# Two heads in two halves of the rows: maxima four at a time, weighing every second slot, other jobs in even slots

## The chip, the cores and the metric

One core of a Trainium2 chip runs the whole program in one launch. The metric is the device time in microseconds of that core. The kernel before took 1429.73 us, the median of three runs (1427.91 to 1433.0). TensorE is the matrix engine, VectorE, ScalarE and GpSimd work on rows, SyncE (SP) issues the DMAs. Matmuls write to PSUM, which has eight banks of 512 f32 columns on 128 partitions.

## The reference

Six blocks run one after the other on x (4 x 256 tokens of 256) with a context of 4 x 4096 tokens of 128. Only the first matters here, attention of x to the context with 16 heads of 16 columns:

```
qh = (q @ Wq + bq) by heads          # q: the normalized x, 256 queries per batch
kh = (k @ Wk + bk) by heads          # k: 4096 context tokens per batch
vh = (v @ Wv + bv) by heads
scores = einsum('bhqd,bhkd->bhqk', qh, kh) / sqrt(16)
attn = softmax(scores)
out = einsum('bhqk,bhkd->bhqd', attn, vh)
```

The five blocks behind it are not touched.

## The kernel before

**Exact products from bf16.** A query or key is split into three bf16 parts (high, middle, low; 16 rows each for a head). Six of the nine products of parts are wanted. They are laid under each other in the rows: 6 x 16 = 96 rows of queries and of keys for a head, read from DRAM by three DMAs for blocks of 48, 32 and 16 rows (`RUNS`, L1019 for keys, L1005 for queries). Two more rows hold minus the maximum of each query, against ones in the keys, so that a matmul of 98 rows gives shifted scores.

**Groups and slots.** A group is two heads of a batch; there are 32. A group has 16 slots, a slot 256 keys (two tiles of 128, `e2`), so there are 512 slots. The numbers t of slots also run from -60 to -1 ahead of them, where keys, queries and first maxima are made. In every slot each engine goes through the same list of work in its own loop over t (`tensor`, `vector`, `scalar`, `gpsimd`, `sync`), with semaphores between them:

- *Scores* (L540): for a tile of keys, two matmuls of 98x256, one for each head, into one bank. Three banks (0 to 2) go round by half-slots. ScalarE's exponential (L783) of 128x512 empties a bank into `probs`.
- *Maxima* (L524): a matmul of 96 rows, 128 queries by 512 keys; VectorE takes the maximum of each row (L685). They run 19 slots ahead, two in a slot, one behind the first scores and one behind the second. When all 32 maxima of a group are there, VectorE finds the shift, TensorE turns it (L614), and ScalarE copies it into the query rows (L846).
- *Weighing* (L559): values (17 columns with a column of ones) times probabilities in f32, in four groups of 32 columns of the array, for four slots at once, in every fourth slot, into bank 3.
- *Other jobs*, at slots that `plan` writes in a table (`due`): keys of the next units projected (L587) and split by GpSimd, values projected (L626), context turned (L578), gathers of a finished group (L645), the shift (L614), and from slot 412 on jobs of the next block ("stream").

**Banks of maxima and jobs.** From slot -1 on a maximum or a job takes the next of banks 4 to 7 in turn (`misc` in `tensor`). Its first matmul waits until the holder before has been emptied, for a maximum by VectorE's `peaked`, for a job mostly by a copy on ScalarE.

**SP** issues loads and stores in the order of the same table; `read keys` brings 1.5 MB for a group into one of three buffers, 31 slots ahead of it.

A matmul in f32 is two instructions in the trace. "96*128" in a row is rows by columns of the weights.

Of the kernel before, what the change touches and what calls it, by code (L numbers as in the profile page):

```python
# [14 lines left out]
P = 128  # L15
# [282 lines left out]
PAIRS = 6  # L298
ROWS = PAIRS * DH
AUG = ROWS + 2  # L300
# [10 lines left out]
HALVES, SUMS = 3, 3  # L311
# [4 lines left out]
class ContextAttention0:  # L316
# [12 lines left out]
    def __init__(self, k, scope):  # L329
# [12 lines left out]
        self.keysT = sb(scope, "keysT", [P, RING, GH, LC], BF16)  # L342
        self.values = [values, sb(scope, "values1", [P, LC // P, H, DH + 1])]
        self.queriesT = sb(scope, "queriesT", [P, 2, P // DH, S], BF16)
# [17 lines left out]
        self.q_dram = k.nc.dram_tensor("q_parts0", (B, P // DH, PARTS, DH, KD, S), BF16).ap()  # L362
# [20 lines left out]
        self.max_made, self.peaked, self.scored, self.exped = sig("max_made"), sig("peaked"), sig("scored"), sig("exped")  # L383
# [6 lines left out]
    def plan(self):  # L390
# [31 lines left out]
        for u in range(2, B * KD):  # L422
            b, m = divmod(u, KD)
            for c in range(CH):
                slot = UNIT * u - 101 + 8 * c
                if m == 0:
                    at(slot - 15, "load ctx", b, c)
                    at(slot, "turn ctx", b, c)
                    at(slot + 6, "save ctx", b, c)
                at(slot + 2, "fill keys", u, c)  # L430
                if c % 2:
                    at(slot + 7, "write parts", u, c // 2)
# [22 lines left out]
    def maxima(self, t):  # L455
# [5 lines left out]
        return range(made(t - 1), made(t))  # L461
# [36 lines left out]
    def tensor(self, e, w):  # L498
# [13 lines left out]
        def find_max(n, now):  # L512
            i, r = divmod(n, MAXES)
            pair, c = self.max_at(n)
            j, t = divmod(pair, QT)
            u, g = divmod(i, UNIT_GROUPS)
            job, let_go = ("max", n), (self.peaked, n)
# [4 lines left out]
            else:  # L522
                w.wait_ge(self.pieces_here[c * self.PIECES // CH], 0)
            e.matmul(ps, self.queriesT[0:ROWS, u % 2, g * GH + j, t * P:(t + 1) * P],  # L524
                     self.keysT[0:ROWS, i % RING, j, c * BANK:(c + 1) * BANK],
                     start=True, stop=True).then_inc(*self.max_made.up(n))

        for t in range(FIRST, TOTAL + 3):
# [16 lines left out]
            if t % 4 == 1 and 5 <= t <= TOTAL + 1:  # L545
                i, p0 = divmod(t - 5, SLOTS)
                b, g = divmod(i, NG)
                w.wait_ge(self.exped, (t - 2, 1))
                for p in range(p0, p0 + 4):
# [5 lines left out]
                for p in range(p0, p0 + 4):  # L555
                    for e2 in range(2):
                        for j in range(GH):
                            quad, kt = e2 * GH + j, 2 * p + e2
                            made = e.matmul(k.bank(SUMS)[32 * quad:32 * quad + DH + 1, 0:S],  # L559
                                            self.values[b % 2][:, kt, g * GH + j, :],  # L560
                                            self.probs[:, (SLOTS * i + p) % RINGP, quad * S:(quad + 1) * S],
                                            start=(p == 0), stop=(p == SLOTS - 1))
                made.then_inc(*self.weighed.up((t - 5) // 4))
            for n in maxima[1:]:
                find_max(n, t)

            for job, *a in self.due.get(t, ()):
# [40 lines left out]
                elif job == "turn shift":  # L608
# [4 lines left out]
                    for pair in range(GH * QT):  # L613
                        made = e.transpose(ps[ROWS:AUG, pair * P:(pair + 1) * P], self.shift_b[:, i % 2, pair, :],  # L614
# [20 lines left out]
    def max_at(self, n):  # L635

        i, r = divmod(n, MAXES)
        return divmod(r, CH) if i else divmod(r, GH * QT)[::-1]
# [30 lines left out]
    def vector(self, e, w):  # L669
# [11 lines left out]
        def peak(n):  # L681
            i, r = divmod(n, MAXES)
            pair, c = self.max_at(n)
            w.wait_ge(self.max_made, n)
# [2465 lines left out]
```

## Time and profile before

| | |
|---|---|
| median of three runs | 1429.73 us (1427.91 to 1433.0) |
| profiled execution, span | 1429.1 us, 28070 instructions |
| slots 0 to 415 | 67.06 to 788.66 us |
| slots 416 to 511 | 788.66 to 963.2 us |
| TensorE, VectorE, ScalarE, GpSimd busy | 96%, 74%, 65%, 20% |
| DMA | 133.19 MB, mean 93 GB/s |

The only time that the profile has of the profiled execution is its span; the median of the runs is 0.6 us above it. A busy share counts matmuls from start to a modelled end, and ends overlap the next starts, so the pitch from start to start says what a matmul costs. In a row of the timeline equal instructions are merged: its second number runs from the first start to the last end. What stands in brackets is the idle time before it and what ended it.

### The profile page before, as it was taken

The numbers are of one execution on the slowest core, as the hardware profiler recorded it, in microseconds if no ns is written. First come the engines' busy times: TensorE is split into PE (matmuls) and PEld (weight loads), VectorE is DVE, ScalarE is ACT, GpSimd is POOL, SyncE is SP. The second block draws the span as 40 slices with busy tenths as digits, with TensorE's granted clock in tenths as the row PEclk, the third lists the DMA queues.
The fourth block names the chain that finished last, engine by engine and source line by source line (L and its number), as shares of the span: only waits on it lengthen the run. The fifth ranks groups of instructions, "written<-read, shape, count | busy, mean of one in ns | idle before, by whom it ended". The sixth has DMA issues, their size and how long they took to land.

```text
span 1429.1 us, 28070 instructions
## 1 busy us (share of the span) xinstructions
PE 1375.6 (96%) x11138; PEld 846.7 (59%) x11138; DVE 1055.1 (74%) x2114; ACT 922.1 (65%) x1899; POOL 287.6 (20%) x321
## 2 busy tenths in 40 slices
PE   7799999999999999999999999999999999989998
PEld 5355555555555545555554556556557999856666
DVE  4787777787777778777778888835876778767757
ACT  5366777767777767777767666672796664448731
POOL 3354222222222222122213100000003100001210
PEclk9899999999999999999999999999999999999999
DMA  6966555346554545655454743002402320347000
GB/s 184 163 145 143 119 118 111 77 102 130 116 127 92 102 84 125 128 115 113 81 97 101 184 73 61 2 1 60 119 18 65 112 67 1 91 112 155 2 1 30
DMA packets 95587, 133.19 MB, mean 93 GB/s; under 512 B 8864, under 2 KB 70944, under 8 KB 89504
## 3 DMA queue, kind: packets, MB, share of 16 engines
q1 hardware_dynamic: 95456, 131.40, 42.3%
q8 instruction: 88, 1.44, 0.5%
q14 instruction: 43, 0.35, 0.1%
HBM read 94.15 MB, written 37.22 MB: 92 GB/s over the span
## 4 chain that ended last, share of the span: by engine, by line
PE 79%; ACT 8%; DVE 8%; DMA 2%; issue 2%; SPq 1%; POOL 0%; DVEq 0%; ACTq 0%
PE psum L559 16%; PE psum L540 13%; PE psum L524 13%; ACT probs L783 4%; PE psum L2132 4%; PE psum L587 3%; PE psum L2106 3%; DVE peaks L685 3%; PE psum L626 3%; PE psum L1226 2%; PE psum L2851 2%; PE psum L1623 1%; PE psum L275 1%; PE psum L2861 1%; PE psum L2814 1%
## 5 line engine op out<-in xcount | busy, mean ns | idle before, releaser
L685 DVE TENSOR_REDUCE peaks<-psum 128x1 f32<-128x512 f32 x1024 | 643.3, 684 | 197.0 <-PE psum L524 196.4
L783 ACT ACTIVATE probs<-psum 128x512 f32<-128x512 f32 x1024 | 529.0, 615 | 83.3 <-PE psum L540 79.4
L524 PE MATMUL psum<-keysT,queriesT 96*128 96x512 bf16 x1024 | 390.1, 384 | 13.2 <-DMA keysT<-key_parts 7.9
L540 PE MATMUL psum<-queriesT,keysT 98*128 98x256 bf16 x2048 | 392.4, 274 | 6.1 <-ACT queriesT L846 2.4
L540 PEld LDWEIGHTS psum<-queriesT,keysT 98*128 98x128 bf16 x2048 | 176.3, 99 | 191.7 <-ACT probs L783 72.1
L559 PE MATMUL psum<-probs,values 128*17 128x256 f32 x4096 | 245.9, 380 | 0.0
L559 PEld LDWEIGHTS psum<-probs,values 128*17 128x17 f32 x4096 | 107.2, 97 | 102.6 <-issue 27.1
L524 PEld LDWEIGHTS psum<-keysT,queriesT 96*128 96x128 bf16 x1024 | 98.6, 96 | 90.9 <-issue 56.1
L918 POOL CAST key_parts<-key_f 128x512 bf16<-128x512 f32 x57 | 34.8, 611 | 518.0 <-ACT key_f L816 511.0
L816 ACT ACTIVATE key_f<-psum,bk 128x512 f32<-128x512 f32 x59 | 40.5, 687 | 120.7 <-PE psum L587 120.6
L587 PE MATMUL psum<-ctxT,wk 128*128 128x512 f32 x128 | 69.5, 625 | 2.4 <-DVE probs L728 0.9
L924 POOL TENSOR_TENSOR key_parts<-key_r,key_parts 128x512 bf16<-128x512 f32 x57 | 66.0, 1158 | 4.5
L920 POOL TENSOR_TENSOR key_r<-key_f,key_parts 128x512 f32<-128x512 f32 x57 | 65.9, 1157 | 4.5
L2132 PEld LDWEIGHTS psum<-ctx_nat,ring 128*128 128x128 f32 x512 | 64.6, 191 | 3.6 <-ACT ring L2267 0.7
L2132 PE MATMUL psum<-ctx_nat,ring 128*128 128x129 f32 x512 | 65.9, 275 | 0.7 <-ACT ring L2267 0.6
L626 PE MATMUL psum<-wv,ctxT 128*128 128x256 f32 x256 | 65.4, 381 | 0.5 <-DVE probs L716 0.4
L1919 ACT ACTIVATE weights<-psum,peaks 128x256 f32<-128x256 f32 x128 | 58.7, 487 | 10.5 <-DVE peaks L1788 10.3
L2106 PE MATMUL psum<-early_weights,ctx_T 128*128 128x256 f32 x256 | 63.2, 380 | 0.0
L857 ACT ACTIVATE values<-psum 128x512 f32<-128x512 f32 x64 | 38.0, 599 | 29.3 <-PE psum L626 28.5
L2257 ACT ACTIVATE ring<-psum 128x512 f32<-128x512 f32 x64 | 37.7, 596 | 29.1 <-PE psum L2106 28.8
L626 PEld LDWEIGHTS psum<-wv,ctxT 128*128 128x128 f32 x256 | 47.9, 190 | 14.0 <-issue 5.5
L2267 ACT ACTIVATE ring<-ring 128x1024 f32<-128x1024 f32 (+1 forms) x36 | 34.6, 962 | 24.3 <-DVE ring L2177 24.1
(315 smaller groups left out, 1662.5 us busy)
## 6 DMA issues: line engine op xcount, KB each, us to landing
keysT<-key_parts SPq DMA_DIRECT2D x31, 768.0 KB, 7.7
key_parts<-key_parts SPq DMA_DIRECT2D x90, 256.0 KB
keysT<-key_parts SPq DMA_DIRECT2D x31, 512.0 KB, 10.1
ctx_nat<-in_ctx_dram SPq DMA_DIRECT2D x32, 256.0 KB, 3.0
keysT<-key_parts SPq DMA_DIRECT2D x31, 256.0 KB, 11.6
ctx_in<-in_ctx_dram SPq DMA_DIRECT2D x24, 256.0 KB, 5.9
ctx_turned<-ctxT SPq DMA_DIRECT2D x24, 256.0 KB, 4.4
ctx_T<-ctx_turned SPq DMA_DIRECT2D x12, 512.0 KB, 3.8
```

Source lines behind the costliest of these rows:

```text
L524: e.matmul(ps, self.queriesT[0:ROWS, u % 2, g * GH + j, t * P:(t + 1) * P], self.keysT[0:ROWS, i % RING, j, c * BANK:(c + 1) * BANK], star ...
L540: made = e.matmul(ps[:, j * S:(j + 1) * S], self.keysT[0:AUG, i % RING, j, kt * P:(kt + 1) * P], self.queriesT[0:AUG, u % 2, g * GH + j, : ...
L559: made = e.matmul(k.bank(SUMS)[32 * quad:32 * quad + DH + 1, 0:S], self.values[b % 2][:, kt, g * GH + j, :], self.probs[:, (SLOTS * i + p) ...
L587: e.matmul(ps, self.wk[:, 0, m * P:(m + 1) * P], self.ctxT[:, c * BANK:(c + 1) * BANK], start=True, stop=True).then_inc(*self.key_made.up( ...
L626: made = e.matmul(ps[:, e2 * D:(e2 + 1) * D], self.ctxT[:, kt * P:(kt + 1) * P], self.wv[:, 0, :], start=True, stop=True)
L685: e.tensor_reduce(self.peaks[:, i % 2, pair, c:c + 1], k.ps(("max", n)), AX.X, ALU.max).then_inc(*self.peaked.up(n))
L783: e.activation(self.probs[:, t % RINGP, e2 * GH * S:(e2 + 1) * GH * S], k.ps(("scores", t, e2)), ACT.Exp).then_inc(*self.exped.up((t, e2)))
L920: e.tensor_tensor(self.key_r[:, :], k_f, part(0), ALU.subtract).then_inc(*w.up(self.split_pool, ("rest",) + key))
L924: e.tensor_tensor(part(2), self.key_r[:, :], part(1), ALU.subtract).then_inc(*w.up(self.split_pool, ("part2",) + key))
L1919: made = e.activation(self.weights[:, (2 * q + i) % self.NR, kt, :], k.ps(("scores3", q, i))[:, kt * S:(kt + 1) * S], ACT.Exp, bias=self.p ...
L2106: made = e.matmul(ps[:, i * S:(i + 1) * S], l.ctx_T[:, b % 2, kt * P:(kt + 1) * P], l.qcT[:, b * S:(b + 1) * S], start=True, stop=True)
L2132: made = e.matmul(k.ps(("weigh4", b, i))[:, 0:C + 1], self.at(n)[:, column:column + P], l.ctx_nat(b % 2)[:, kt, :], start=(kt == 0), stop= ...
```

## The change

Names: `MAIN` and `REST` are two planes of the key and query rows. Head j of a group lies in rows 64j to 64j+63. `MAIN` holds four of the six products (64 rows), `REST` the other two (32 rows) and the two shift rows (34 in all).

- Scores: for each tile and head one matmul of 64 rows and one of 34, added up in PSUM; a bank now belongs to a head (both tiles of a slot) and no longer to a tile (both heads). Three banks as before.
- Maxima: the 64 rows of `MAIN` only (the maximum need not be exact, it cancels); four in every even slot, head 0 and 1 in turn, behind all scores.
- Weighing: two slots at once, in every odd slot (`BLOCK`).
- Table: key projections, context and their writes one slot later or earlier, so that they fall on even slots; value projections every eighth slot instead of every sixth.
- The shift is copied by two instructions, one for each head.
- DMAs: keys of a group six of 32 rows each (three before); query parts are written in five copies (three before) and read by four DMAs (three before).

```diff
-            for e2 in range(2):
-                if 0 <= t < TOTAL:
-                    kt, n = 2 * p + e2, (2 * t + e2) % HALVES
-                    ps = banks.use(n, w, ("scores", t, e2), (self.exped, (t, e2)))
-                    for j in range(GH):
-                        made = e.matmul(ps[:, j * S:(j + 1) * S], self.keysT[0:AUG, i % RING, j, kt * P:(kt + 1) * P],
-                                        self.queriesT[0:AUG, u % 2, g * GH + j, :], start=True, stop=True)
-                    made.then_inc(*self.scored.up((t, e2)))
-                if maxima and not e2:
-                    find_max(maxima[0], t)
+                ps = {}
+                for e2 in range(2):
+                    kt = 2 * p + e2
+                    for plane, rows in ((MAIN, HALF), (REST, TALL)):
+                        for j in range(GH):
+                            if j not in ps:
+                                ps[j] = banks.use(SCORES[(2 * t + j) % len(SCORES)], w, ("scores", t, j), (self.exped, (t, j)))
+                            own = slice(j * HALF, j * HALF + rows)
+                            made = e.matmul(ps[j][:, e2 * S:(e2 + 1) * S], self.keysT[own, plane, i % RING, kt * P:(kt + 1) * P],
+                                            self.queriesT[own, plane, u % 2, g, :], start=(plane == MAIN), stop=(plane == REST))
+                            if e2 and plane == REST:
+                                made.then_inc(*self.scored[j].up((t, j)))
+            for n in maxima:
+                find_max(n, t)
...
+        if t < 0:
+            return range(made(t - 1), made(t))
+        return range(made(t - 1), made(t + 1)) if t % 2 == 0 else range(0)
...
-                slot = UNIT * u - 101 + 8 * c
+                slot = UNIT * u - 100 + 8 * c
...
-                at(SLOTS * NG * b - 97 + 6 * p, "make values", b, p)
+                at(SLOTS * NG * b + (8 * p - 96 if p < 12 else (-6, 0, 2, 8)[p - 12]), "make values", b, p)
...
-        for block, run in RUNS:
-            e.dma_start(self.keysT[block * DH:(block + run) * DH, i % RING, :, keys],
-                        self.key_dram[u, g * GH:(g + 1) * GH, PARTS - run:PARTS, :, keys].rearrange(
-                            "j i d n -> (i d) j n")).then_inc(*landed.up(key))
+        for j in range(GH):
+            for row, plane, first in ((0, MAIN, 1), (LOW, MAIN, 1), (0, REST, 0)):
+                e.dma_start(self.keysT[j * HALF + row:j * HALF + row + LOW, plane, i % RING, keys],
+                            self.key_dram[u, g * GH + j, first:first + 2, :, keys].rearrange("i d n -> (i d) n")).then_inc(
+                    *landed.up(key))
```

TensorE, a steady piece with a value projection, before. L540 are scores, L524 maxima, L559 weighing, L626 values; `exped` is ScalarE's exponential, `peaked` VectorE's maximum:

```order
944 L524 MATMUL psum<-keysT,queriesT 128x512 [waits peaked]
945 L540 MATMUL psum<-queriesT,keysT 128x256 [waits exped]
946 L540 MATMUL psum<-queriesT,keysT 128x256
947 L559 MATMUL psum<-probs,values 17x256 x16
948 L524 MATMUL psum<-keysT,queriesT 128x512 [waits peaked]
949 L626 MATMUL psum<-wv,ctxT 128x256 [waits peaked]
950 L626 MATMUL psum<-wv,ctxT 128x256
951 L540 MATMUL psum<-queriesT,keysT 128x256 [waits exped]
952 L540 MATMUL psum<-queriesT,keysT 128x256
953 L524 MATMUL psum<-keysT,queriesT 128x512 [waits peaked]
```

The same kind of piece now (L548 scores, L529 maxima, L568 weighing, L634 values):

```order
694 L548 MATMUL psum<-queriesT,keysT 128x256 [waits exped] x2
695 L548 MATMUL psum<-queriesT,keysT 128x256 x6
696 L529 MATMUL psum<-keysT,queriesT 128x512 [waits peaked] x3
697 L529 MATMUL psum<-keysT,queriesT 128x512 [waits key_kept]
698 L634 MATMUL psum<-wv,ctxT 128x256 [waits peaked]
699 L634 MATMUL psum<-wv,ctxT 128x256
700 L548 MATMUL psum<-queriesT,keysT 128x256 [waits exped] x2
701 L548 MATMUL psum<-queriesT,keysT 128x256 x6
702 L568 MATMUL psum<-probs,values 17x256 x8
703 L548 MATMUL psum<-queriesT,keysT 128x256 [waits exped] x2
```

The single maxima between scores have become a run of four behind a slot's eight score matmuls, the job stands right behind the four, and weighing has half the matmuls and comes twice as often. Both runs of the job wait for `peaked`, but four turns of the banks back is now the first of the four maxima just issued.

SP ahead of slot 0, from the last piece of group 0 to the keys of group 2, before (L1019 keys, L980 ones, L983 x):

```order
34 L1019 DMA keysT<-key_parts 48x2x1024 [waits parts3_out]
35 L1019 DMA keysT<-key_parts 32x2x1024
36 L1019 DMA keysT<-key_parts 16x2x1024
37 L1019 DMA keysT<-key_parts 48x2x4096
38 L1019 DMA keysT<-key_parts 32x2x4096
39 L1019 DMA keysT<-key_parts 16x2x4096
40 L980 DMA keysT<-in_const_dram 1x128x96 x2
41 L983 DMA values<-in_x_dram 128x6x256
```

and now (L1036 keys, L991 ones, L995 x):

```order
34 L1036 DMA keysT<-key_parts 32x1024 [waits parts3_out]
35 L1036 DMA keysT<-key_parts 32x1024 x5
36 L1036 DMA keysT<-key_parts 32x4096 x6
37 L991 DMA keysT<-in_const_dram 1x128x48 x4
38 L995 DMA values<-in_x_dram 128x6x256
```

Each read of keys has twice as many DMAs, with the same places in the row.

## Rows read from the trace of the kernel before

**Rows 1.** The page: busy time of the engines, and the granted clock in 40 slices

```profile
PE 1375.6 (96%) x11138; PEld 846.7 (59%) x11138; DVE 1055.1 (74%) x2114; ACT 922.1 (65%) x1899; POOL 287.6 (20%) x321
...
PEclk9899999999999999999999999999999999999999
```

**Rows 2.** Windows: length, busy by engine, clock, DMA share, GB/s

```profile
67.06:788.66 721.60, 713.80 (x6425) 386.45 (x6423) 549.87 (x1008) 519.90 (x1015) 201.34 (x229) 1.00 0.55 112
...
788.66:963.20 174.54, 168.35 (x1555) 102.32 (x1554) 130.94 (x277) 114.95 (x223) 12.43 (x12) 1.00 0.30 62
```

**Rows 3.** Timeline (start, length, engine) of scores and maxima, around 504 and 509 to 512

```profile
504.35 0.11 PEld L540 LDWEIGHTS psum<-queriesT,keysT 98*128 98x128 bf16 x2 [0.27 <-ACT probs L783]
...
508.60 0.38 PE L540 MATMUL psum<-queriesT,keysT 98*128 98x256 bf16 x2
...
509.04 0.38 PE L540 MATMUL psum<-queriesT,keysT 98*128 98x256 bf16 x2
...
509.26 0.38 PE L524 MATMUL psum<-keysT,queriesT 96*128 96x512 bf16 x1
...
509.48 0.38 PE L540 MATMUL psum<-queriesT,keysT 98*128 98x256 bf16 x2
...
509.94 0.39 PE L540 MATMUL psum<-queriesT,keysT 98*128 98x256 bf16 x2
...
511.04 1.88 DVE L685 TENSOR_REDUCE peaks<-psum 128x1 f32<-128x512 f32 x3
```

**Rows 4.** Timeline of one weighing of four slots

```profile
511.90 0.39 PE L540 MATMUL psum<-queriesT,keysT 98*128 98x256 bf16 x2
...
512.22 1.92 PE L559 MATMUL psum<-probs,values 128*17 128x256 f32 x32
...
514.07 0.39 PE L524 MATMUL psum<-keysT,queriesT 96*128 96x512 bf16 x1
```

**Rows 5.** Timeline: a key projection (two matmuls), a transpose of context (four)

```profile
501.09 1.02 PE L587 MATMUL psum<-ctxT,wk 128*128 128x512 f32 x2
...
340.68 0.60 PE L578 MATMUL psum<-const,ctx_in 128*128 128x128 f32 x4
```

**Rows 6.** Timeline: f32 matmuls alone, then in pairs of row groups; their durations

```profile
1000.81 1.03 PE L1701 MATMUL psum<-early_weights,w_oT 128*128 128x256 f32 x4
...
1001.77 1.13 PE L1623 MATMUL psum<-qT,kT 32*128 32x256 f32 x8
...
L1623 PEld LDWEIGHTS psum<-qT,kT x256: 181/185/333, 978.4 to 1067.7; 32*128 32x128 f32 x128
...
L1623 PE MATMUL psum<-qT,kT x256: 374/374/791, 978.4 to 1068.1; 32*128 32x256 f32 x128
```

**Rows 7.** Timeline: an exponential, a maximum's matmul and its reduction

```profile
503.69 0.61 ACT L783 ACTIVATE probs<-psum 128x512 f32<-128x512 f32 x1
...
507.50 0.39 PE L524 MATMUL psum<-keysT,queriesT 96*128 96x512 bf16 x1
...
507.93 0.69 DVE L685 TENSOR_REDUCE peaks<-psum 128x1 f32<-128x512 f32 x1 [1.07 <-PE psum L524]
```

**Rows 8.** Timeline: a reduction and the load that waits for its bank

```profile
48.04 0.68 DVE L685 TENSOR_REDUCE peaks<-psum 128x1 f32<-128x512 f32 x1
...
48.77 0.10 PEld L524 LDWEIGHTS psum<-keysT,queriesT 96*128 96x128 bf16 x1 [0.50 <-DVE peaks L685]
```

**Rows 9.** Waits: total, times, longest

```profile
PEld psum L645 <- DVE peaks L685: 8.0, 17, 1.6
```

**Rows 10.** Lines, 67.06 to 788.66: count, busy, mean ns, idle before

```profile
L685 DVE TENSOR_REDUCE peaks<-psum 128x1 f32<-128x512 f32 x831 | 522.5, 684 | 168.2 <-PE psum L524 167.9
...
L783 ACT ACTIVATE probs<-psum 128x512 f32<-128x512 f32 x830 | 426.7, 617 | 37.5 <-PE psum L540 34.5
```

**Rows 11.** Timeline: the first maximum of group 1, and SP's reads

```profile
62.10 1.98 PE L524 MATMUL psum<-keysT,queriesT 96*128 96x512 bf16 x4 [6.41 <-DMA keysT<-key_parts]
...
517.31 1.25 SPq L1019 DMA_DIRECT2D keysT<-key_parts  x3
```

More of the change, by code:

```diff
@@ L297 @@
 RUNS = ((0, 3), (3, 2), (5, 1))
-PAIRS = 6
-ROWS = PAIRS * DH
-AUG = ROWS + 2
+KEY_AT = (1, 2, 0)
+QUERY_AT = ((2, 3), (0, 1), (4,))
+HALF = P // 2
+MAIN, REST = 0, 1
+LOW = 2 * DH
+TALL = LOW + 2
 NG = H // GH
@@ L512, in find_max @@
         def find_max(n, now):
-            i, r = divmod(n, MAXES)
-            pair, c = self.max_at(n)
-            j, t = divmod(pair, QT)
+            i, j, qt, c = self.max_at(n)
             u, g = divmod(i, UNIT_GROUPS)
+            own = slice(j * HALF, (j + 1) * HALF)
             job, let_go = ("max", n), (self.peaked, n)
@@ L523, in find_max @@
                 w.wait_ge(self.pieces_here[c * self.PIECES // CH], 0)
-            e.matmul(ps, self.queriesT[0:ROWS, u % 2, g * GH + j, t * P:(t + 1) * P],
-                     self.keysT[0:ROWS, i % RING, j, c * BANK:(c + 1) * BANK],
-                     start=True, stop=True).then_inc(*self.max_made.up(n))
+            e.matmul(ps, self.queriesT[own, MAIN, u % 2, g, qt * P:(qt + 1) * P],
+                     self.keysT[own, MAIN, i % RING, c * BANK:(c + 1) * BANK],
+                     start=True, stop=True).then_inc(*self.max_made[j].up(n))
         for t in range(FIRST, TOTAL + 3):
@@ L637, in max_at @@
         i, r = divmod(n, MAXES)
-        return divmod(r, CH) if i else divmod(r, GH * QT)[::-1]
+        step, j = divmod(r, GH)
+        qt, c = divmod(step, CH) if i else divmod(step, QT)[::-1]
+        return i, j, qt, c
     def gather(self, e, w, ps, i):
@@ L845, in scalar @@
                     w.wait_ge(self.shiftT_made, i)
-                    e.activation(self.queriesT[ROWS:AUG, u % 2, g * GH:(g + 1) * GH, :].rearrange("p h n -> p (h n)"),
-                                 k.ps(("shiftT", i)).bitcast(BF16)[ROWS:AUG, 0:GH * S], ACT.Copy).then_inc(
-                        *self.shiftT_kept.up(i))
+                    for j in range(GH):
+                        own = slice(j * HALF + LOW, j * HALF + TALL)
+                        e.activation(self.queriesT[own, REST, u % 2, g, :], k.ps(("shiftT", i)).bitcast(BF16)[own, 0:S],
+                                     ACT.Copy).then_inc(*self.shiftT_kept.up(i if j else ("first", i)))
                 elif job == "make values":
@@ L978, in sync @@
                     n, first, last = CONST_COLS["ones"]
-                    for r in range(ROWS, AUG):
-                        e.dma_start(self.keysT[r:r + 1, :, :, :].rearrange("o r h n -> o (r h n)").bitcast(F32).rearrange(
-                            "o (p n) -> o p n", p=P), io["const"][:, first:last].unsqueeze(0)).then_inc(*self.ones_in.up(0))
+                    for r in (LOW, LOW + 1, HALF + LOW, HALF + LOW + 1):
+                        e.dma_start(self.keysT[r:r + 1, REST, :, :].rearrange("o r n -> o (r n)").bitcast(F32).rearrange(
+                            "o (p n) -> o p n", p=P), io["const"][:, first:(first + last) // 2].unsqueeze(0)).then_inc(
+                            *self.ones_in.up(0))
                 elif job == "load x":
@@ L989, in sync @@
                     if i >= RING:
-                        w.wait_ge(self.scored, (SLOTS * (i - RING + 1) - 1, 1))
+                        for j in range(GH):
+                            w.wait_ge(self.scored[j], (SLOTS * (i - RING + 1) - 1, j))
                     self.read_keys(e, i, slice(0, LC), self.keys_here[i % RING], i)
@@ L1002, in sync @@
                     if u >= 2:
-                        w.wait_ge(self.scored, (UNIT * (u - 1) - 1, 1))
-                    for block, run in RUNS:
-                        e.dma_start(self.queriesT[block * DH:(block + run) * DH, u % 2, :, :],
-                                    self.q_dram[b, :, 0:run, :, m, :].rearrange("h i d n -> (i d) h n")).then_inc(
-                            *self.rows_here[u % 2].up(u))
+                        for j in range(GH):
+                            w.wait_ge(self.scored[j], (UNIT * (u - 1) - 1, j))
+                    for plane, rows, parts in ((MAIN, HALF, slice(0, 4)), (REST, LOW, slice(3, 5))):
+                        for j in range(GH):
+                            e.dma_start(self.queriesT[j * HALF:j * HALF + rows, plane, u % 2, :, :],
+                                        self.q_dram[b, j::GH, parts, :, m, :].rearrange("h i d n -> (i d) h n")).then_inc(
+                                *self.rows_here[u % 2].up(u))
                 elif job == "load output weights":
```

67 lines of the change are left out of this document (33 added, 34 removed).

## The prediction

> **What bounds the kernel now.** I read the page's shares first: TensorE is busy 96% of the span at full clock, and no other engine is over 74% [rows 1]. The reader should see that "busy" hides waits, so I next cut the span into stretches. The 416 slots from 67.06 to 788.66 us take 721.60 us, 1.735 us a slot, and the last 96 slots 174.54 us [rows 2]. In the first of these TensorE is busy 713.80 us, VectorE 549.87, ScalarE 519.90. The change works here; the 466 us behind 963.2 run code that it does not touch.
>
> Then the timeline of a few slots. A maximum follows every pair of scores, and both take 0.22 us where nothing waits (509.04 to 509.26 to 509.48). From the fourth half-slot on, the pitch grows from 0.44 to 0.49 us, because scores wait for an exponential [rows 3]. Eight half-slots then run from 508.60 to 512.13 us (the second matmul of the pair at 511.90 starts 0.39 - 0.27 = 0.12 later and streams 0.11). Weighing follows: its first load starts at 512.22, 0.09 after the last column, and the next maximum starts at 514.07. So four slots' weighing costs 1.95 us, of which eight waves of 0.216 are work and 0.22 are the two changes of array layout [rows 4]. With the eighth maximum (0.22) four slots cost 3.53 + 0.22 + 1.95 = 5.70 us. 104 such blocks are 593 us, and the other jobs 123 us (52 key projections at 2 x 0.43, 48 value projections at 4 x 0.216, 24 transposes of context and 25 gathers at 4 x 0.11, 26 turns of the shift at 0.32, few others; the counts are the order's, the pitches (1.02 - 0.59) and (0.60 - 0.27) / 3) [rows 5]. That is 716 of 721.60; the method is 0.8% short.
>
> **The change on TensorE.** *Maxima.* 128x512 stays, but the two heads lie in rows 0 to 63 and 64 to 127. Do such pairs run side by side? The trace has pairs in different 32-row groups: eight f32 matmuls start at 1001.77 and end at 1002.90. Less one duration (0.374) the last starts at 1002.53; with the first wave delayed 0.10 by its load, that is 0.216 a pair, where single f32 matmuls of 256 columns have the same pitch ((1.03 - 0.38) / 3) [rows 6]. So I take a pair at the price of one: four maxima cost 0.44 instead of 0.87 us, 0.43 us saved in two slots. *Scores.* Four matmuls a slot become eight, in four waves of 0.11: 0.455 us against 0.45. Nothing saved. *Weighing.* Every second slot: four waves 0.86, plus 0.09 before and 0.11 behind [rows 4]; two layout changes more in four slots, 0.11 us a slot.
>
> *The wait of scores.* Three banks hold scores, and slot t+1 needs for its second head the bank of slot t's first head. Before, a half-slot reused the bank of three half-slots earlier, with maxima in between. Now both heads of a slot finish together. Set the first score load of an even slot at 0: columns end at 0.46; the last wave starts at 0.35, is complete at 0.62, ScalarE starts 0.04 later and takes 0.60 (one exponential 0.61), and TensorE goes on 0.05 after its end (503.69 + 0.61 to 504.35) [rows 3, 7]: 1.31. The maxima fill 0.46 to 0.90, and 0.41 us stay empty. Odd scores then end at 1.77, weighing at 2.85, when the next wait is long over. A pair of slots costs 2.86 us with the first load, against 5.70 / 2 = 2.85 before: the 0.43 saved is spent on a wait of 0.41, and the second layout change is paid by the score waits of before that go.
>
> *The wait of the other jobs.* They take turns with the maxima in four banks. Four maxima at once take all four, so a job in an even slot needs the bank of the first of these very maxima. The first maximum starts at 0.47, is complete at 0.86, VectorE starts 0.04 later (507.50 + 0.39 to 507.93) for 0.69 us, and its bank comes free 0.05 behind it (48.04 + 0.68 to 48.77) [rows 7, 8]: load at 1.63. An f32 load without cover costs 0.10 [rows 6]. Then 0.86 of work and 0.11 to change the layout back: scores at 2.70 instead of 1.31, +1.39, for a job that cost 0.86. Before, the maximum whose bank it took was two slots old; only 8.0 us of such a wait (17 gathers) are in the trace [rows 9]. Transposes or a gather: 1.63 + 0.10 + 0.44 + 0.11 - 1.31 = +0.97; both +1.40; keys and shift +1.81. By the order, of 208 even slots below 416, 48 have values, 25 keys, 25 keys and shift, 25 transposes or a gather, 12 both, one the shift alone (+0.74). That is 67 + 35 + 45 + 24 + 17 + 1 = 189; jobs in odd slots behind weighing 6.
> Sum: 208 x 2.86 + 189 + 6 = 790; with the 0.8% that the method lacks, 796 against 721.6: **+74**. The last 48 pairs: 137 + 30 + 12 (19 of their jobs lie in odd slots, which need no fresh peak), 180 against 174.5: **+5**.
>
> **VectorE and ScalarE.** Maxima back to back come every 0.60 us on VectorE ((1.88 - 0.68) / 2), four take 2.4 us, under 2.86; exponentials cost ScalarE at most 0.51 (426.7 / 830), four 2.1 [rows 3, 10]. Neither bounds. The shift's copy becomes two, on 32 groups, some 0.3 us each, beside idle ScalarE; if not hidden, 10 us.
> The Trainium skill, "TensorEngine Tiling (Array Packing)", section PSUM Bottleneck, warns that tiling speeds up TensorE but not the emptying of PSUM. By that rule alone two slots could not go under VectorE's 2.4 us. The trace agrees that VectorE keeps 0.60 a maximum, but my sum stays above that floor, so here it is latency and not throughput that takes the gain.
>
> **Transfers.** A read of keys becomes six DMAs of 32 rows instead of three, the same bytes. An issue holds SP some 0.43 us (three in 1.25), so +1.3 us a read, with 11 slots to spare in the steady part. Ahead of slot 0 it counts: the program stands 6.41 us at 62.10 for keys of group 1, and in front of that read 12 + 2 + 1 issues are added (pieces, copies of queries, row reads), partly in SP's idle time [rows 11]. Bounds 0 and 18 x 0.43 = 8 us; I take **+2**.
>
> Total: 1429.1 + 74 + 5 + 2 = 1510; the median of the runs shown (1429.73) lies 0.6 above the profiled span, so 1511 us, 5.7% slower.
>
> **Rivals.** *The row halves do not hide their weight loads.* Nothing here shows bf16 loads in 64-row halves. One takes 0.10 us now, just under a wave of 0.11; if two queue up, or if each costs the 0.19 of an f32 load [rows 6], a wave takes 0.19. Scores: 8 waves a pair of slots, +0.08 each, +0.63; x 256 = +160: 1670 us. Against it: the f32 pairs' loads overlap fully. Chance 10%. The Trainium skill, "TensorE: Matmul & The Clock Gate", section Weight-path perf modes, ties the fast load to 128 columns and a type other than f32, and excludes column tiling, not row tiling; by it the wave stays at 0.11, though no run here shows it. Without the page I would give the same chance, since the rows alone leave the step open.
> *The job's wait does not form* (the first peak is done before the job comes, because the scores' wait covers it): jobs fit the empty 0.41, a job ends at 0.90 + 0.10 + 0.86 + 0.11 = 1.97. That is 0.73 less for 135 + 17 jobs: 1511 - 111 = 1400 us, faster. It decides if VectorE frees a bank within 0.43 us of a maximum's start; the rows make it 1.16. Chance 4%.
> *Neither wait forms:* TensorE pays columns and layout changes only, 0.46 + 0.44 + 0.46 + 1.08 = 2.44 a pair: 0.42 x 256 = 107 off the pairs, and each job costs its work and two changes of layout (0.86 + 0.21 = 1.07 instead of 1.39), 0.32 x 163 = 52 off: about 1352 us. Chance 4%, as the exponential's 0.60 is measured. It would also show if the two heads' waves did not end together.
> *No change in sum*: the waits are half as long: 1430 to 1450, 4%.
>
> **Numbers.** Forecast 78%, its own range 1470 to 1570 (layout change 0.09 to 0.20 [rows 4, 6], some 580 more of them; head 0 to 8; shift copies). Range for 8 in 10: 1430 to 1600; it leaves out 1670 and the two faster cases. 0.3% (4 us) is about what a measurement tells from no change: faster 9%, same 2%, slower 89%.
>
> **What would show it.** Even score slots: loads of the second head idle some 0.4 us, released by the exponential. Every job behind four maxima: its load idle some 0.7 us, released by VectorE's peak. Score waves at 0.11 with two starts a few ns apart; weigh blocks of 16 matmuls 1.08 apart end to end. Slots 0 to 415 in about 796 us. I am wrong if score waves are at 0.2, or if loads behind the maxima start at once.

## The result, and the profile after

| | before | after |
|---|---|---|
| median of the runs | 1431.37 us (4 runs, 1427.91 to 1433.46) | 1519.34 us (4 runs, 1514.61 to 1523.07) |
| ratio, 95% interval | | 1.061 (1.059 to 1.064): slower |
| profiled execution, span | 1429.1 us | 1512.8 us |
| ahead of slot 0 | 67.06 us | 63.81 us |
| slots 0 to 415 | 721.6 us | 795.9 us |
| slots 416 to 511 | 174.5 us | 190.4 us |
| behind slot 511 | 465.9 us | 462.7 us |

The forecast was 1511 us in a range of 1430 to 1600, with 89% on slower. The four stretches differ by -3.3, +74.3, +15.9 and -3.2 us; that is 83.7 us, and 1512.8 - 1429.1 is the same. The medians differ by 88.0, since the profiled execution was the fastest of the four (1514.61 us, with the span of 1512.8).

The page's shares and clock (beside [rows 1]) show the cost as idle time on TensorE, while its work got smaller:

```profile
PE 1362.5 (90%) x13186; PEld 781.0 (52%) x13186; DVE 1052.6 (70%) x2114; ACT 962.3 (64%) x1931; POOL 286.8 (19%) x321
...
PEclk9899999999999999999999999999999999999999
```

The windows of the same stretches as [rows 2]:

```profile
63.81:859.70 795.89, 705.30 (x8105) 338.38 (x8104) 547.28 (x1009) 556.25 (x1043) 200.96 (x229) 1.00 0.42 103
859.70:1050.10 190.40, 169.84 (x1926) 92.41 (x1922) 130.58 (x275) 119.45 (x227) 12.41 (x12) 1.00 0.23 57
```

In slots 0 to 415 TensorE is busy 705 us (before 714) in 796 (before 722). VectorE does what it did, 547 us, far from full. The granted clock is 1.00 in both stretches, the level of 2.4 GHz, so the clock is no part of the cost.

**A pair of slots without a job.** The timeline, beside [rows 3, 4]. L548 are scores, L529 maxima, L568 weighing, L793 the exponential:

```profile
515.43 0.62 PE L548 MATMUL psum<-queriesT,keysT 64*128 64x256 bf16 x8
...
515.89 0.59 PE L529 MATMUL psum<-keysT,queriesT 64*128 64x512 bf16 x4
...
516.14 2.29 ACT L793 ACTIVATE probs<-psum 128x512 f32<-128x512 f32 x4 [0.51 <-PE psum L548]
...
516.32 0.27 PE L548 MATMUL psum<-queriesT,keysT 64*128 64x256 bf16 x1
516.79 0.33 PEld L548 LDWEIGHTS psum<-queriesT,keysT 64*128 64x128 bf16 x7 [0.59 <-ACT probs L793]
...
517.34 1.06 PE L568 MATMUL psum<-probs,values 128*17 128x256 f32 x16
518.33 0.34 PEld L548 LDWEIGHTS psum<-queriesT,keysT 64*128 64x128 bf16 x8 [0.42 <-ACT probs L793]
```

Eight score matmuls take 0.62 us; less one duration (0.27) that is 0.35, three pitches of 0.117 and no seven: two row halves run side by side at the column pace. Four maxima take 0.59, less 0.38 one pitch of 0.21: also two at a time. So the pairs came as forecast. Then one score matmul of the odd slot goes into the free bank, and the other seven wait until 516.79, 0.05 behind the end of the first exponential (516.14 + 0.60). Between 516.32 and 516.79 TensorE streams that one score, 0.11 us, and stands for the other 0.36. The pair is over after 518.33 - 515.43 = 2.90 us, forecast 2.86.

The last row is a trap for readers: its 0.42 has the exponential's name, but the loads of weighing simply ended early. Its sixteen matmuls run in four waves of four. In the trace the last of them starts at 518.02 and streams for one pitch, 0.216, so the columns end at 518.23, and the load comes 0.09 later, as for the same change of layout in [rows 4].

**A pair with a value projection** (L634), the timeline beside [rows 7, 8]; L695 is VectorE's maximum:

```profile
511.21 0.62 PE L548 MATMUL psum<-queriesT,keysT 64*128 64x256 bf16 x8
...
511.67 0.59 PE L529 MATMUL psum<-keysT,queriesT 64*128 64x512 bf16 x4
...
512.08 2.48 DVE L695 TENSOR_REDUCE peaks<-psum 128x1 f32<-128x512 f32 x4 [1.73 <-PE psum L529]
512.83 0.73 PEld L634 LDWEIGHTS psum<-wv,ctxT 128*128 128x128 f32 x4 [1.06 <-DVE peaks L695]
512.83 1.13 PE L634 MATMUL psum<-wv,ctxT 128*128 128x256 f32 x4 [0.56 <-DVE peaks L695]
513.89 0.34 PEld L548 LDWEIGHTS psum<-queriesT,keysT 64*128 64x128 bf16 x8 [0.33 <-issue]
```

The job loads at 512.83, that is 1.62 behind the start of the pair (forecast 1.63), 0.06 behind the end of the first of the four peaks (512.08 + 0.69), and the odd scores start at 2.68 (forecast 2.70).

The waits of the whole program, of which [rows 9] showed the nearest before:

```profile
DVE peaks L695 <- PE psum L529: 279.3, 217, 4.8
...
PEld psum L548 <- ACT probs L793: 148.8, 320, 0.9
...
PEld psum L634 <- DVE peaks L695: 48.6, 48, 1.1
PEld psum L594 <- DVE peaks L695: 46.5, 52, 1.1
```

48 value projections and 52 key projections (L594) now wait for a peak. The load queue stands 1.0 and 0.9 us before each; counted from the last column of the four maxima (511.67 + 2 x 0.216 = 512.10, load at 512.83) it is 0.7. VectorE, for which they wait, itself stands 279 us for maxima: it idles between batches of four and is late within them.

### The profile page after: what moved, and what is told of

Read it like the earlier page. It is cut to its first block, busy times and chain, and to the rows that moved or that the text cites. A ratio compares the mean times of both kernels' runs of the same rounds, so it can differ in the third digit from the quotient of the medians.

```text
span 1512.8 us, 32416 instructions
## 1 busy us (share of the span) xinstructions
PE 1362.5 (90%) x13186; PEld 781.0 (52%) x13186; DVE 1052.6 (70%) x2114; ACT 962.3 (64%) x1931; POOL 286.8 (19%) x321
## 4 chain that ended last, share of the span: by engine, by line
PE 70%; DVE 16%; ACT 10%; issue 2%; DMA 0%; POOL 0%; SPq 0%; ACTq 0%; DVEq 0%; POOLq 0%
PE psum L548 16%; PE psum L568 14%; DVE peaks L695 11%; PE psum L594 4%; PE psum L634 4%; ACT probs L793 4%; PE psum L2149 3%; PE psum L2123 3%; PE psum L529 3%; PE psum L1243 2%; PE psum L2868 2%; ACT key_f L826 1%; PE psum L655 1%; ACT queriesT L858 1%; PE psum L2878 1%
## 5 line engine op out<-in xcount | busy, mean ns | idle before, releaser
L695 DVE TENSOR_REDUCE peaks<-psum 128x1 f32<-128x512 f32 x1024 | 637.1, 683 | 280.4 <-PE psum L529 279.3
L793 ACT ACTIVATE probs<-psum 128x512 f32<-128x512 f32 x1024 | 555.5, 595 | 175.2 <-PE psum L548 159.7
L548 PE MATMUL psum<-queriesT,keysT 64*128 64x256 bf16 (+1 forms) x4096 | 348.5, 273 | 25.2 <-ACT probs L793 21.0
L548 PEld LDWEIGHTS psum<-queriesT,keysT 64*128 64x128 bf16 (+1 forms) x4096 | 170.7, 95 | 235.7 <-ACT probs L793 148.8
L568 PE MATMUL psum<-probs,values 128*17 128x256 f32 x4096 | 270.8, 382 | 0.0
L529 PE MATMUL psum<-keysT,queriesT 64*128 64x512 bf16 x1024 | 172.3, 379 | 10.4 <-DMA keysT<-key_parts 4.7
L568 PEld LDWEIGHTS psum<-probs,values 128*17 128x17 f32 x4096 | 94.1, 96 | 105.2 <-issue 54.9
L594 PE MATMUL psum<-ctxT,wk 128*128 128x512 f32 x128 | 74.4, 665 | 25.7 <-DVE peaks L695 23.6
L634 PE MATMUL psum<-wv,ctxT 128*128 128x256 f32 x256 | 70.8, 402 | 25.4 <-DVE peaks L695 24.9
L529 PEld LDWEIGHTS psum<-keysT,queriesT 64*128 64x128 bf16 x1024 | 59.6, 94 | 43.1 <-DVE peaks L695 25.8
L634 PEld LDWEIGHTS psum<-wv,ctxT 128*128 128x128 f32 x256 | 43.9, 189 | 56.1 <-DVE peaks L695 48.6
```

What stands on the lines that cost most here:

```text
L529: e.matmul(ps, self.queriesT[own, MAIN, u % 2, g, qt * P:(qt + 1) * P], self.keysT[own, MAIN, i % RING, c * BANK:(c + 1) * BANK], start=Tr ...
L548: made = e.matmul(ps[j][:, e2 * S:(e2 + 1) * S], self.keysT[own, plane, i % RING, kt * P:(kt + 1) * P], self.queriesT[own, plane, u % 2, g ...
L594: e.matmul(ps, self.wk[:, 0, m * P:(m + 1) * P], self.ctxT[:, c * BANK:(c + 1) * BANK], start=True, stop=True).then_inc(*self.key_made.up( ...
L634: made = e.matmul(ps[:, e2 * D:(e2 + 1) * D], self.ctxT[:, kt * P:(kt + 1) * P], self.wv[:, 0, :], start=True, stop=True)
L695: e.tensor_reduce(self.peaks[:, i % 2, j * QT + qt, c:c + 1], k.ps(("max", n)), AX.X, ALU.max).then_inc(*self.peaked.up(n))
L793: e.activation(self.probs[:, t % RINGP, 2 * j * S:(2 * j + 2) * S], k.ps(("scores", t, j)), ACT.Exp).then_inc(*self.exped.up((t, j)))
```

## Experiments

All were made from the kernel after. Ratios are to the kernel before, run on the same chip beside them. Lengths of pairs are medians from the first score matmul of an even slot to that of the next, in slots 0 to 415:

| pair with | forecast | after | e1 | e3 | e6 | e9 |
|---|---|---|---|---|---|---|
| no job | 2.86 | 2.90 | 2.90 | 3.12 | 2.93 | 3.12 |
| value projection | 4.25 | 4.22 | 3.95 | 3.59 | 3.58 | 3.62 |
| key projection | 4.25 | 4.21 | 3.95 | 3.58 | 3.58 | 3.58 |
| keys and shift | 4.67 | 4.42 | 4.15 | 3.79 | 4.21 | 3.79 |
| transposes | 3.83 | 3.75 | 3.48 | 3.12 | 3.52 | 3.11 |
| gather | 3.83 | 3.72 | 3.45 | 3.09 | 3.52 | 3.12 |
| transposes and gather | 4.26 | 4.32 | 3.85 | 3.52 | 3.94 | none |
| slots 0 to 415, us | 796 | 795.9 | 755.5 | 719.5 | 727.8 | 710.4 |

The medians hide one kind of pair. At the start of a group 21 of the 48 value projections take 4.63 and not 4.22, because the group's first scores wait for ScalarE's copy of the shift into the query rows. In the kernel after:

```profile
PEld psum L548 <- ACT queriesT L858: 10.6, 25, 0.4
```

and in the kernel before:

```profile
PEld psum L540 <- ACT queriesT L846: 11.1, 21, 0.6
```

So this wait is no cost of the change. It stands at 10.6 us in e1, e3 and e8 too, and is gone from the lists of e2, e6 and e9.

**e1_half_peaks: a shorter peak, all else the same.**

```diff
-            e.tensor_reduce(self.peaks[...], k.ps(("max", n)), AX.X, ALU.max)
+            e.tensor_reduce(self.peaks[...], k.ps(("max", n))[:, 0:BANK // 2], AX.X, ALU.max)
```

> The changed kernel, but VectorE's maximum reads only the first 256 of the 512 columns (it leaves out half of the keys of each maximum). Theory (a job behind four maxima waits for the first peak): the first peak is done about 0.27 us earlier, so every job in an even slot (163 of them) starts 0.27 us earlier and pairs of slots without a job stay at 2.86 us: 163 x 0.27 = 44 us less, about 1475 us. Rival (TensorE's columns and layout changes set the time, VectorE has 16% idle and is off the path): no change, 1519 us.

Measured: 1471.8 us, ratio 1.028 (1.025 to 1.032). The timeline of a value projection:

```profile
505.42 0.70 PE L529 MATMUL psum<-keysT,queriesT 64*128 64x512 bf16 x4
505.83 1.42 DVE L695 TENSOR_REDUCE peaks<-psum 128x1 f32<-128x256 f32 x4 [3.15 <-PE psum L529]
506.31 0.73 PEld L634 LDWEIGHTS psum<-wv,ctxT 128*128 128x128 f32 x4 [0.69 <-DVE peaks L695]
```

The first peak takes (1.42 less three pitches of 0.33) 0.42 us and no longer 0.69, and the job starts 0.48 behind VectorE's start where it was 0.75. Every kind of pair with a job behind the four maxima loses 0.27 (with both jobs 0.47), the pair without one nothing. So TensorE waits for the length of one peak, as the forecast had it, though VectorE is busy only 70% of the kernel after, and 53% of this one.

**e2_odd_jobs: keys, values and context one slot earlier, behind weighing.**

```diff
-                slot = UNIT * u - 100 + 8 * c
+                slot = UNIT * u - 101 + 8 * c
-                    at(slot + 6, "write parts", u, c // 2)
+                    at(slot + 7, "write parts", u, c // 2)
-                at(SLOTS * NG * b + (8 * p - 96 if p < 12 else (-6, 0, 2, 8)[p - 12]), "make values", b, p)
+                at(SLOTS * NG * b + (8 * p - 97 if p < 12 else (-7, -1, 1, 7)[p - 12]), "make values", b, p)
```

> The changed kernel with key and value projections and the transposes of context one slot earlier, so that they follow weighing in odd slots and not four fresh maxima; shift and gathers stay in even slots. Theory: such a job costs about 1.05 us (work 0.86, layout in and out 0.19) instead of 1.39, 0.34 x 122 = 41 us less, but a shift or a gather that now stands alone behind the maxima has the wait of its own, +0.3 x 25 and +0.5 x 12, 14 us: together 27 us less, about 1492 us. Rival (the peak's wait is not what a job costs): 1519 us or more, since a job in an odd slot no longer fills the empty 0.41 us of an even one.

Measured: 1489.2 us, ratio 1.042 (1.039 to 1.046); slots 0 to 415 in 762.8. A value or key pair is 3.96 (4.22 before the move), one with transposes 3.46 (3.75). The timeline shows the job right behind weighing:

```profile
508.25 1.06 PE L568 MATMUL psum<-probs,values 128*17 128x256 f32 x16
509.23 0.73 PEld L634 LDWEIGHTS psum<-wv,ctxT 128*128 128x128 f32 x4 [0.42 <-DVE peaks L695]
...
510.29 0.34 PEld L548 LDWEIGHTS psum<-queriesT,keysT 64*128 64x128 bf16 x8 [0.33 <-issue]
```

The load comes 0.98 behind weighing's start, as scores' does (518.33 - 517.34 above): the "0.42 <-DVE" is the trap once more, the peak is no longer waited for. The job costs 510.29 - 509.23 = 1.06. The gain is only 0.26 because in this place no stall pays for the work: the wait for the exponential stays whole in the same pair. Both waits are real, and undoing one leaves the other. Of the 33 us that slots 0 to 415 gain, up to 10.6 are the wait for the shift's copy, which has gone from this kernel's list as well, and not the job's wait.

**e3_two_maxima: two maxima in every slot, no batch of four.**

```diff
-        if t < 0:
-            return range(made(t - 1), made(t))
-        return range(made(t - 1), made(t + 1)) if t % 2 == 0 else range(0)
+        return range(made(t - 1), made(t))
```

> The changed kernel with two maxima (one pair of heads) in every slot instead of four in every second one; all else as changed. Theory: behind only two maxima a job's bank is a slot old, so a job starts at once in the empty time before the odd scores (0.44 us instead of 1.39 for keys and values, nothing for transposes and gathers), while a pair of slots without a job grows from 2.86 to 3.08, because only one pair of maxima is left to fill the scores' wait: 208 x 3.08 + 66 = 707 us for slots 0 to 415 instead of 796, and about 9 less behind: about 1421 us, faster than the kernel before. Rival (layout changes are the loss): the same number of layout changes, so no gain, 1519 or more.

Measured: 1433.8 us (10 runs), ratio 1.0033 (1.0015 to 1.0051), 13 above what I expected; a pair without a job takes 3.12 for the expected 3.08, which is 8 of them. Its waits:

```profile
PEld psum L546 <- ACT probs L791: 204.1, 414, 1.1
...
PEld psum L527 <- DVE peaks L693: 16.7, 25, 2.3
...
PEld psum L632 <- DVE peaks L693: 8.6, 27, 0.3
```

The waits of value and key projections for peaks fell from 95.1 us to 13.9 (8.6 for L632, 5.3 for L592). Scores now wait in both slots of a pair (414 times, 0.49 each), since only two maxima stand in front of the second head's scores; so a pair without a job grows by 0.22, and one with a projection shrinks by 0.63. This edit alone takes 76 us off slots 0 to 415 (795.9 to 719.5), where the change had cost 74. The batch of four is what made the change slow; the row halves, the weighing of two slots and the layout changes are in this kernel too.

**e4_block4: weighing of four slots at once again, maxima still four.** `BLOCK = 4` for `BLOCK = 2`.

> The changed kernel with weighing of four slots in every fourth slot, as before the change. Theory (the wait of scores in three banks): two layout changes of four go (-0.22 us in four slots), but where an odd slot has no weighing the next scores wait for the exponential, 1.31 us from score to score: 6.34 us for four slots without jobs instead of 5.72, +0.6 x 128 = 79, about 1598 us. Rival (the changes of layout cost what was gained): 128 x 0.22 = 28 us less, 1491 us.

Measured: 1615.0 us, ratio 1.131 (1.126 to 1.136), slots 0 to 415 in 870.9. Half of the layout changes around weighing are saved, and slots 0 to 415 still take 75 us more: the weighing of every second slot covered the next score wait. In a pair without it the timeline shows one wait behind the other:

```profile
509.02 0.33 PEld L548 LDWEIGHTS psum<-queriesT,keysT 64*128 64x128 bf16 x7 [0.53 <-ACT probs L793]
...
510.22 0.33 PEld L548 LDWEIGHTS psum<-queriesT,keysT 64*128 64x128 bf16 x7 [0.62 <-ACT probs L793]
```

A slot of 0.46 us of columns lasts 510.22 - 509.02 = 1.20, two exponentials of 0.60.

**e5_four_banks: a fourth bank for scores, three for maxima and jobs.** `SCORES = (0, 1, 2, 7)` and the turn of `misc` over banks 4 to 6.

> The changed kernel with four banks for scores (0, 1, 2, 7) and three (4, 5, 6) for maxima and jobs; maxima stay four at a time. Theory: the scores' wait goes, but the fourth maximum now needs the bank of the first, 1.16 us after that one's start, and the odd scores stand behind it: a pair of slots costs 0.46 to 1.86 for the even one, then 0.46 + 1.08, 3.40 us instead of 2.86, and a job costs 1.4 as before: + 0.54 x 256 = 138, about 1657 us. Rival (the exponential is the wait that counts): the 0.41 us in every pair goes, 256 x 0.41 = 105 less, about 1414 us.

Measured: 1648.8 us (2 runs, 1644.1 to 1653.6), ratio 1.151 (1.144 to 1.158). Its waits:

```profile
PEld psum L529 <- DVE peaks L695: 274.4, 280, 2.5
ACT probs L793 <- PE psum L548: 233.6, 308, 3.7
```

With three banks the fourth maximum of a batch waits for the first's peak, and a pair without a job takes 3.37 (expected 3.40). This is the same mechanism with the maxima themselves as the followers, 280 times.

**e6_four_two and e7_four_two_b4: four score banks, three others, two maxima a slot;** the edits of e5 and e3 together, e7 with weighing of four slots as well.

> Four banks for scores, three for maxima and jobs, and two maxima in every slot; weighing every second slot as changed. Theory: neither the exponential nor a fresh peak is waited for, except in pairs without a job, where the fourth maximum waits 0.26 us or more for the first: 2.93 us such a pair, 3.5 with keys or values, 3.1 with transposes or a gather: about 690 us for slots 0 to 415 instead of 796, about 1395 us in all. Rival (the row halves give nothing on this chip beyond what layout changes cost): 1430 or more, as with three banks and two maxima.

> The same with weighing of four slots in every fourth. Theory: with the scores' wait gone the layout changes are what is left: two of four go, 0.22 us in four slots, at least 28 us less than with weighing every second slot; VectorE's 4.8 us for the maxima of four slots and its wait in a weighing of 1.95 us bound it from below at about 5.4 us for four slots: between 1300 and 1365 us. Rival (three banks for maxima are too few when four slots of scores follow each other): the fourth slot's maxima wait for VectorE and nothing is gained, 1395 us.

Measured: e6 1442.9 us (8 runs), ratio 1.007 (1.005 to 1.010); e7 1491.8 us, 1.041 (1.038 to 1.045). Both expectations missed. In e6 the pair without a job is what I had worked out, 2.93; but pairs with the shift, transposes or a gather cost 0.40 to 0.43 more than in e3. Its time is that of the rival (1430 or more), but the rival's reason, that the row halves give nothing, is not what the waits show. Its waits, and two rows of its timeline:

```profile
PEld psum L546 <- ACT probs L791: 121.7, 288, 0.8
...
PEld psum L527 <- DVE peaks L693: 78.0, 151, 1.7
```

```profile
484.05 0.89 PE L527 MATMUL psum<-keysT,queriesT 64*128 64x512 bf16 x2
484.55 0.09 PEld L527 LDWEIGHTS psum<-keysT,queriesT 64*128 64x128 bf16 x1 [0.51 <-DVE peaks L693]
```

Two maxima that should take 0.38 take 0.89: the second needs a bank whose peak is not done. The fourth score bank took 82 us off the wait for exponentials (204.1 to 121.7), and the missing bank for maxima put 61 on the wait for peaks (16.7 to 78.0). In e7, where weighing comes in every fourth slot only, maxima wait for peaks 238 times (151 in e6), and slots 0 to 415 take 766.0 us:

```profile
PEld psum L527 <- DVE peaks L693: 117.7, 238, 2.2
```

I had priced the bank given and not enough the one taken. In sum slots 0 to 415 take 8 us more than in e3: what the moved bank took off one wait it put on the other and on the jobs. No other split of the banks was run.

**e8_serial_maxima: the maxima of a batch in one row half.** Sixteen of head 0, then sixteen of head 1, so that no two neighbours lie in different halves (but in two of a group's eight batches, which cross from one head to the next).

```diff
+        if i:
+            j, step = divmod(r, QT * CH)
+            qt, c = divmod(step, CH)
         return i, j, qt, c
```

> The changed kernel with another order of maxima from group 1 on: first the sixteen of head 0, then the sixteen of head 1, so that the four of a slot lie in the same half of the rows and follow each other (0.87 us instead of 0.44). Theory: they stand beside the scores' wait, which ends at 1.31 us, and a job behind them waits for the first peak until 1.63 us anyway: at most 0.05 to 0.1 us in the 65 pairs without a job, 1519 to 1526 us. Rival (the time of maxima on TensorE is on the path, and running them side by side is what the change brings): + 0.43 x 256 = 110, about 1629 us.

Measured: 1522.7 us, ratio 1.064 (1.061 to 1.067), level with the kernel after (its ratio 1.059 to 1.064). The timeline of a batch:

```profile
517.57 0.62 PE L548 MATMUL psum<-queriesT,keysT 64*128 64x256 bf16 x8
517.92 0.20 PEld L529 LDWEIGHTS psum<-keysT,queriesT 64*128 64x128 bf16 x2
518.03 0.38 PE L529 MATMUL psum<-keysT,queriesT 64*128 64x512 bf16 x1
518.03 0.09 PEld L548 LDWEIGHTS psum<-queriesT,keysT 64*128 64x128 bf16 x1
518.03 0.28 PE L548 MATMUL psum<-queriesT,keysT 64*128 64x256 bf16 x1
518.24 0.81 PE L529 MATMUL psum<-keysT,queriesT 64*128 64x512 bf16 x3
...
518.93 0.33 PEld L548 LDWEIGHTS psum<-queriesT,keysT 64*128 64x128 bf16 x7 [0.37 <-ACT probs L796]
```

The maxima now take four waves instead of two, and the seven scores come 518.93 - 517.57 = 1.36 behind the start, exactly as in the kernel after (516.79 - 515.43). That is the forecast's sentence "the 0.43 saved is spent on a wait" as an experiment: take the saving away, and slots 0 to 415 take 797.2 us for 795.9, where the rival wanted some 90 more.

**e9_spread: e3 with the jobs spread.** A fill of keys comes 6 slots behind its projection (before 2), writes 8 (6), `normalize` two slots later, and the last four value projections at slots 0, 4, 8, 12, so that two jobs seldom meet.

```diff
-                at(slot + 2, "fill keys", u, c)
+                at(slot + 6, "fill keys", u, c)
-                at(SLOTS * i + SLOTS + 4, "normalize", i)
+                at(SLOTS * i + SLOTS + 6, "normalize", i)
-                at(SLOTS * NG * b + (8 * p - 96 if p < 12 else (-6, 0, 2, 8)[p - 12]), "make values", b, p)
+                at(SLOTS * NG * b + (8 * p - 96 if p < 12 else (0, 4, 8, 12)[p - 12]), "make values", b, p)
```

> Two maxima in every slot (as in the run with three banks and two maxima), and the table spread so that no even slot has two jobs: key projections four slots later, gathers two slots later, the last four value projections of a batch at slots 0, 4, 8, 12. Theory: a pair with one transpose, gather or shift costs what an empty one costs (3.12), so the 25 shifts beside keys (3.79 - 3.59) and the 12 doubles (3.52 - 3.12) save 10 us: about 1424 us, just faster than the kernel before. Rival (the jobs add up wherever they stand): no change, 1434 us.

Measured: 1427.2 us (12 runs), ratio 0.9976 (0.9960 to 0.9992), the only kernel below the one before, by 0.24%, clear of the noise of these runs but small. Slots 0 to 415 take 9.1 us less than in e3, by kinds of pairs 4.8 from the doubles and 4.1 from the shifts beside keys, as expected; another 3.3 come from value projections at a group's start (3.73 for 3.89), where the wait for the shift's copy is gone, and pairs with other jobs or none give some 3 back. The timeline of a pair with the shift's turn (L620):

```profile
505.57 0.62 PE L546 MATMUL psum<-queriesT,keysT 64*128 64x256 bf16 x8
...
506.34 0.28 PE L620 MATMUL psum<-ident_b,shift_b 128*2 128x128 bf16 x4
...
506.55 1.00 PE L546 MATMUL psum<-queriesT,keysT 64*128 64x256 bf16 x8
506.93 0.33 PEld L546 LDWEIGHTS psum<-queriesT,keysT 64*128 64x128 bf16 x7 [0.29 <-ACT probs L791]
...
508.70 0.48 PEld L546 LDWEIGHTS psum<-queriesT,keysT 64*128 64x128 bf16 x8 [0.42 <-issue]
```

The pair is 3.13 long, as one without a job. A small job alone (four matmuls of 0.11 or less) fits into the wait for the exponential and is free, in the table 3.11 and 3.12 for transposes and a gather against 3.12 for no job; two together stand out (3.52 in e3), so spreading them pays.

## Why the prediction was right, and where its terms were off

- *The saving.* Maxima in pairs at the price of one: shown (0.21 for the second pair). Scores at 0.117 a wave: shown. The rival of loads that don't hide (a wave of 0.19, 1670 us) is refuted by the same rows.
- *The wait of scores* (0.41 empty behind the maxima, pair 2.86): shown, pair 2.90. The 0.05 is the hand-over to ScalarE: the last wave starts at 515.78 and is complete at 516.05, and the exponential starts at 516.14, 0.09 later and not 0.04. e8 shows that the maxima's saved time bought nothing.
- *The sum of slots 0 to 415* (790 + 6 for what the method lacks, measured 795.9) hit a tenth by luck. The terms, over 2.86 a pair: value projections 74 (forecast 67), keys 34 (35), keys and shift 41 (45), transposes or a gather 22 (24), both 17.5 (17), jobs in odd slots 10 (6), pairs without a job 3 (0). The largest term off, the value projections, is the wait of a group's first scores for the shift's copy, 21 times 0.41; the forecast had that copy down as "beside idle ScalarE; if not hidden, 10 us" and left it out of the sum. The kernel before has the same wait (11.1 us), so the 0.8% by which the method fell short there (716 of 721.60) stands for part of it without naming it.
- *The wait of jobs* (load at 1.63, scores at 2.70): shown to 0.02 us, in one pair and in the medians, and by e1 as a wait for one peak's length. The rivals that needed it absent (1400 and 1352 us) fall with it.
- *The shift's turn* behind keys: 0.21 and not 0.42, 25 times, 5 us too much. In e9 its four matmuls stand for 506.55 - 506.34 = 0.21 with scores right behind them, so it pays no change of layout, which my 0.42 had put on it.
- *Slots 416 to 511, forecast +5, measured +15.9: the mis-sized term.* The 48 pairs make 47 x 2.90 + 1.7 = 138 us (forecast 137), so the jobs took 52 where I had 30 + 12. The timeline of an odd slot with a job of eight matmuls (L1243):

```profile
1020.08 1.06 PE L568 MATMUL psum<-probs,values 128*17 128x256 f32 x16
1021.07 1.59 PEld L1243 LDWEIGHTS psum<-early_weights,xnT 128*128 128x128 f32 x8 [0.42 <-issue]
...
1022.99 0.45 PEld L548 LDWEIGHTS psum<-queriesT,keysT 64*128 64x128 bf16 x9 [0.33 <-issue]
```

  It costs 1022.99 - 1021.07 = 1.92, for eight pitches of 0.216 = 1.73; the 0.19 is 0.10 for the first load, which nothing covers, and 0.09 for the change of layout behind the job. Even if "19 of their jobs lie in odd slots, which need no fresh peak" had all of these at their bare work, that is 19 x 0.19 = 3.6 of the 10 us. In even slots such a job costs 2.18, and some jobs there wait for the same peaks:

```profile
PEld psum L1243 <- DVE peaks L695: 6.6, 8, 1.1
PEld psum L1236 <- DVE peaks L695: 5.5, 7, 1.2
```

  The forecast does not say how its 30 and 12 are made up, so how the other 6 us divide stays open.

- *Ahead of slot 0, forecast +2, measured -3.3.* The first maxima of group 1 waited 6.41 us for their keys in [rows 11], and now 1.90:

```profile
58.98 1.00 PE L529 MATMUL psum<-keysT,queriesT 64*128 64x512 bf16 x3 [1.90 <-DMA keysT<-key_parts]
```

  The added DMA issues did not cost the 2 us, nor the forecast's bound of 8. That they made the keys earlier is not shown: in the profiles of the nine kernels made from this one, whose DMAs ahead of slot 0 are the same, that wait is 0.93 to 4.90 us and slot 0 starts between 64.8 and 67.5 us. Most of the 3.3 us may be the scatter of single executions.
- *Behind slot 511*, where no code differs, 3.2 us less, with a granted clock of 0.99 against 0.98 in the windows. In the other profiles the same code takes 462 to 468 us from the last score on, so this too is scatter and no part of the change.

The forecast's weak place was not a mechanism. A cost taken from one place (a job, a turn of the shift) was carried over to places with another neighbour, where the changes of layout count differently, and one wait that the trace of the kernel before showed, for the shift's copy, was in no term of the sum.

The Trainium skill, "TensorEngine Tiling (Array Packing)", section PSUM Bottleneck, says that the emptying of PSUM does not speed up with tiling. The trace agrees: a peak alone takes 0.69 us and peaks in a row come every 0.60 ((2.48 - 0.69) / 3), as before. e1 adds how it bites here: through the length of one peak in front of a job, with VectorE idle 30% of the time.

On the rival of the weight loads: loads of 64 rows take 0.09 to 0.10 us, as long as those of 98 rows before, so row halves cost them nothing. That the fast load excludes column tiling, which the forecast puts beside this, stands in the Trainium skill in "TensorEngine Tiling (Array Packing)", section Restrictions, and not in the section named there. No run here shows it.

## What to carry to other kernels

Work that is made faster in front of a wait shifts into the wait, so ask of each saving what the next instruction needs, from which bank, and how long the chain matmul, hand-over, emptying, reuse is (here 1.36 us for scores, 1.62 for a job). A batch that fills all the banks of its turn makes its follower wait for its first member (four maxima in four banks here). One bank of room is no guarantee: two maxima a slot waited 16.7 us for peaks in four banks (e3) and 78.0 in three (e6). A bank moved from one turn to the other has a price on both sides, and small jobs belong, one at a time, into a wait that stands anyway.

## What the runs showed of the hardware that was not expected

- Matmuls in different row halves need not start in the order of the program. In e8 the load and the matmul of a score (L548 at 518.03) start beside the first maximum, ahead of three maxima (L529 from 518.24) that stand before it in the program. By the starts in the trace a score overtakes at least one maximum in 40 of the 185 batches whose four maxima lie in one half, and in 37 of the 93 in rows 64 to 127, where the score of head 0 has the other half. So a serial batch in one half can leave the other usable.
- Two loads of 64 rows in bf16, one in each half, start 3 to 4 ns apart, take 0.09 to 0.10 us each and hide wholly under a wave of 0.117 (after, 515.553 and 515.556 under the wave from 515.551).
- The mean granted clock of the same kernel after differs between executions, 0.994, 0.993, 0.985 and 0.988, and its spans go with it: 1512.8, 1514.6, 1521.3 and 1520.5 us. That is 0.6%, as much as the smaller differences above, and only many runs (10 for e3, 12 for e9) tell these apart.
